# Cross-attention of a perceiver layer: the value product ahead of the scores on TensorE, low part and sums ahead of the scaled scores on VectorE

## The reference, cut to what matters

```
x = x + xattn(layernorm(x), ctx, lens, Wq, Wk, Wv, Wo, q_norm_w, k_norm_w)     # x [32, 64, 128], ctx [32, 1601, 128]

qh = rms_norm(heads(q @ Wq), q_norm_w);  kh = rms_norm(heads(kv @ Wk), k_norm_w);  vh = heads(kv @ Wv)   # 16 heads of 64
scores = where(mask, einsum('bhld,bhsd->bhls', qh, kh) / 8, NEG_INF)
o = einsum('bhls,bhsd->bhld', softmax(scores), vh)
return o.reshape(b, l, 1024) @ Wo
```

## Time and profile before

| what | value |
|---|---|
| median of 3 runs | 2734.34 us (2728.91 to 2734.52) |
| the profiled execution, its own time | 2733.9 us |
| its span, first to last instruction | 2732.0 us |
| PE busy | 2497.1 us, 91% |
| PEld / DVE / ACT / POOL busy | 78% / 76% / 51% / 45% |
| TensorE's granted clock, mean | 0.966 of full |

### The profile page before, as it was taken

How to read it: one execution, slowest core, us unless ns; L and a number is a source line. 1 busy time by engine, 2 the same in 40 slices (tenths; PEclk the granted TensorE clock), 3 DMA queues, 4 the chain that set the end, 5 groups by cost and what they waited for, 6 DMA issues and landing times. The chain is left out here.

```text
span 2732.0 us, 53851 instructions
## 1 busy us (share of the span) xinstructions
PE 2497.1 (91%) x16440; PEld 2131.2 (78%) x16440; DVE 2063.5 (76%) x3018; ACT 1395.2 (51%) x3048; POOL 1239.8 (45%) x638
## 2 busy tenths in 40 slices
PE   5979999999999999999999999999999868799842
PEld 3657888888888888888888888888888757677622
DVE  5679888888888888888888888888888501666567
ACT  4644555555555555555555555555555330465530
POOL 2313555555555555555555555555555630122245
PEclk7999999999999999999999999999999979899975
DMA  2331111111111111111111111111111035000000
GB/s 82 139 111 34 42 41 48 40 40 40 52 40 41 48 40 40 39 40 40 48 40 41 41 52 40 40 48 41 40 39 36 21 129 203 1 0 0 1 0 16
DMA packets 136733, 128.14 MB, mean 47 GB/s; under 512 B 9776, under 2 KB 119280, under 8 KB 136560
## 3 DMA queue, kind: packets, MB, share of 16 engines
q1 hardware_dynamic: 132080, 110.78, 12.9%
q10 hardware_dynamic: 4608, 16.78, 1.5%
HBM read 92.91 MB, written 34.60 MB: 47 GB/s over the span
## 5 line engine op out<-in xcount | busy, mean ns | idle before, releaser
L360 POOL TENSOR_TENSOR probs<-scores,best_all 128x1024 f32 (+2 forms) x416 | 985.4, 2373 | 950.2 <-DVE best L704 942.8
L886 PEld LDWEIGHTS u_ps<-rows,probs 128*128 128x128 f32 x6656 | 806.1, 192 | 53.4 <-issue 9.2
L689 DVE SCALAR_TENSOR_TENSOR scores<-s_ps,mask,rrms 128x512 f32 (+2 forms) x832 | 618.6, 745 | 272.8 <-PE s_ps L761 272.5
L886 PE MATMUL u_ps<-rows,probs 128*128 (+1 forms) x6656 | 811.0, 275 | 13.4 <-ACT probs L545 11.0
L545 ACT ACTIVATE probs<-probs 128x1024 f32<-128x1024 f32 (+1 forms) x416 | 439.6, 1057 | 421.4 <-POOL probs L360 417.5
L506 ACT ACTIVATE squares<-k_ps 128x512 f32<-128x512 f32 (+1 forms) x832 | 464.0, 597 | 201.0 <-PE k_ps L761 145.6
L665 DVE TENSOR_REDUCE ssq<-squares 128x16 f32<-128x1024 f32 (+1 forms) x416 | 502.1, 1207 | 0.0
L704 DVE TENSOR_TENSOR best<-best,scores 128x1024 f32<-128x1024 f32 (+1 forms) x352 | 467.7, 1329 | 0.3
L759 PE MATMUL k_ps<-w_hi,cT_hi 128*128 128x512 f32 (+1 forms) x832 | 362.5, 436 | 11.6 <-DVE cT_lo L659 11.6
L759 PE MATMUL s_ps<-q_hi,cT_hi 128*128 (+2 forms) x832 | 361.9, 435 | 3.5 <-ACT best_all L511 1.4
L761 PE MATMUL k_ps<-w_hi,cT_lo 128*128 128x512 f32 (+1 forms) x832 | 327.7, 394 | 0.0
(11 more groups left out here) (199 smaller groups left out, 2576.7 us busy)
## 6 DMA issues: line engine op xcount, KB each, us to landing
stage<-in_ctx SPq DMA_DIRECT2D x384, 64.0 KB, 1.7
rows<-in_ctx SPq DMA_DIRECT2D x32, 768.0 KB
queries<-probs SPq DMA_DIRECT2D x16, 1024.0 KB, 4.0
q_plain<-queries SPq DMA_DIRECT2D x32, 512.0 KB, 3.2
u_transposed<-uT_sb ACTq DMA_DIRECT2D x32, 512.0 KB, 2.7
a_uT<-u_transposed SPq DMA_DIRECT2D x16, 1024.0 KB, 4.7
a_wqkv<-in_L_attn_w_qkv SPq DMA_DIRECT2D x1, 1536.0 KB, 9.4
stage<-in_ctx SPq DMA_DIRECT2D x32, 32.5 KB
```

The lines of the kernel that those rows point to most:

```text
L360: pool.tensor_tensor(probs[0:r, slot_of(c, PRING), :], scores_at(b, c), best_all[0:r, bass.ds((b % 2) * HL, HL)], ALU.subtract).then_inc(s ...
L689: dve.scalar_tensor_tensor(out=scores_at(p, c, h * HALF, HALF).rearrange("p (h l) -> p h l", l=L), in0=s_ps[h][0:r, :].rearrange("p (h l) ...
L886: last = pe.matmul(u_ps[g // 3][:, at:at + UW], probs[0:r, s, g * P:(g + 1) * P], rows, start=(c == 0 and g % 3 == 0), stop=(c == NC - 1), ...
```

## The change

In PE's step `values` moves ahead of `score`. In DVE's step `split_lo` and then `sum_squares` move ahead of both `scale`, which now follow each other. The instructions and their waits are the same, and so are all buffers.

```diff
@@ DVE, step @@
                 if on.rows and c == 0:
                     keep_best(p - 1, n - 1, NC - 1)
+                if on.turn:
+                    split_lo(n + TURN_AHEAD, at_step(p, c, TURN_AHEAD)[1])
+                if on.keys:
+                    sum_squares(n + KEYS_AHEAD, at_step(p, c, KEYS_AHEAD)[1])
                 if on.scores:
                     scale(p, n, c, 0)
-                if on.turn:
-                    split_lo(n + TURN_AHEAD, at_step(p, c, TURN_AHEAD)[1])
-                if on.scores:
                     scale(p, n, c, 1)
-                if on.keys:
-                    sum_squares(n + KEYS_AHEAD, at_step(p, c, KEYS_AHEAD)[1])
@@ PE, step @@
                     turn(later, n + TURN_AHEAD, tile)
-                if on.scores:
-                    score(p, n, c)
                 if on.values:
                     vc = (c - LAG) % NC
                     values(p - 1 if c >= LAG else p - 2, n - NC - LAG, vc)
+                if on.scores:
+                    score(p, n, c)
```

## The result

| | before | after |
|---|---|---|
| median of 4 runs each | 2734.43 us (2728.91 to 2737.25) | 2916.56 us (2913.4 to 2920.85) |
| ratio | | 1.067, 95% interval 1.0648 to 1.0691 |
| the profiled execution / its span | 2733.9 / 2732.0 us | 2913.4 / 2911.5 us |
| granted clock, mean | 0.966 | 0.968 |

A forecast was written before the change was run, and what follows sets the result against it. PE, full in the dense loop, was taken as the bound. Stalls of 5.06 us in each of 29 batches (146.7), plus 0.6, 0.9 and 9.2, summed to 157.4 us, giving 2891 us; range 2838 to 2930 us.

The forecast's parts named there:

- The full PE with its gain of 0: Dense loop: PE is busy 500.00 of 500 us and the change removes no instruction, so nothing is gained.
- The third rival: Switch between product and value matmuls: not slower, some 0.09 us dead time saved a step, 37 us, 2697 us; 2%.
- the signs: PE in the loop: exponential row some 110 us, over 170 entries; busy about 92%; stalled `values` at K+2.0 to 2.3.
- E - 1.29: Value product in PE's step: stall in us from an exponential ending at E, with deadline 1.50 and restart 0.21.
- The four saves: ACT in c = 3, 4, 8, 9: saves delay the exponential; stalls 0.69 + 0.62 + 0.63 + 0.54 = 2.48 us a batch.
- the second rival: Plain steps stall too: hand-overs cost 0.05 us more each, 0.2 in six free steps, 35 us more, 2926 us; 15%.
- the first: Rival: only the saves and the division stall, 3.52 us a batch, 2842 us; 12%.
- The restart: PE's value product after a wait: 0.14 us to the first matmul plus 0.07 over 16; 0.21, bounds 0 to 0.21.
- VectorE's half at no cost: DVE's plain step: its moves cost nothing, covered by 0.87 us of slack before `scale` 0 can start.
- The reading as a wait for the port: DVE, c = 10: `keep_best` waits for POOL's `q_lo`, then runs whole; 2891 us, against 2907 with shared bandwidth.
- The stretch without `project`: Rest of p = 31: the chain, not PE, bounds; steps go from 3.81 to 4.65 us, 9.2 us over 11 steps.
- chain of 7.6: Rest of p = 31: us from `score` of c to `values` of c+2; with 1.7 added, two steps take 9.3.

## Why the prediction was right, and where it was too low

**What bounds and what gives way.** The full PE with its gain of 0 was right. Only c = 7 got shorter, by 0.11, and most of that is a boundary that moved. The two kernels with the later value product show it without stalls: c = 8, 9 and 10 take 5.04 + 5.11 + 4.76 = 14.91 us under PE's new order and 5.12 + 5.11 + 4.67 = 14.90 under the old one, so what the step with the first transposes gains the plain step behind them gives back. The third rival, a dead time that the switch between products would save, has nothing for it. Of the signs, the row behind the exponential had its 172 entries but 68.3 us, not 110, and PE's busy share fell to 95%, not 92: a modelled end of a matmul hides part of each stall. `values` came at K+2.0 to 2.1 in five of the seven steps, but at K+2.38 in c = 0 and 2.64 in c = 6.

**The deadline.** E - 1.29 held; E is the end of the exponential in its step, counted from K, the start of `project`. ACT's rows of c = 3 and c = 6:

```profile
1250.16 0.60 ACT L511 ACTIVATE best_all<-x_ps 128x512 f32 x1 [2.85 <-PE x_ps L863]
1250.66 1.05 ACT L545 ACTIVATE probs<-probs 128x1024 f32<-128x1024 f32 x1
...
1266.13 1.06 ACT L545 ACTIVATE probs<-probs 128x1024 f32<-128x1024 f32 x1 [2.96 <-POOL probs L360]
1267.09 2.15 ACT L519 ACTIVATE u_sb<-u_ps,inv_sum 128x128 f32<-128x128 f32 x8
```

In c = 3 the save pushes the exponential to 1251.71, K+1.98 as forecast, and the step grew 0.64 for 0.69. The four saves together cost 2.48 (0.64 + 0.67 + 0.60 + 0.57) for 2.48, c = 0 0.90 for 0.87. Each of the four is off by up to 0.05. The plain steps c = 5, 10 and 12, whose margin was put at 0.03, stayed at 4.68: the second rival is out, and so is the first, which gave 2842, as six exponentials a batch do wait.

**The restart.** It was the unknown price, put at 0.21 between 0 and 0.21. The first matmul follows the end of the exponential by 0.14 (1251.71 to 1251.85) and 16 take 2.05 for the 1.95 of c = 5: 0.24. From what the Trainium skill (TensorE: Matmul & The Clock Gate, "The mechanism") says on weight loads pulled ahead of matmuls in flight the forecast had drawn that it could be free, and the time 2848. The trace shows that it is not free here, where the weights themselves are what is awaited.

**VectorE's half at no cost: the step that failed.** The slack of 0.87 was right as a sum over the step, but the chain does not ask for a sum. DVE's rows of c = 10, 1 and 5, and POOL's of c = 10 and 5:

```profile
1219.44 1.70 DVE L704 TENSOR_TENSOR best<-best,scores 128x1024 f32<-128x1024 f32 x1
...
1239.67 0.68 DVE L708 TENSOR_REDUCE best_row<-x_ps 128x4 f32<-128x512 f32 x1
...
1260.45 1.43 DVE L689 SCALAR_TENSOR_TENSOR scores<-s_ps,mask,rrms 128x512 f32 x2 [0.47 <-PE s_ps L760]
1262.00 1.23 DVE L704 TENSOR_TENSOR best<-best,scores 128x1024 f32<-128x1024 f32 x1
```

```profile
1217.66 2.41 POOL L390 TENSOR_TENSOR q_lo<-q_plain,q_hi 128x1024 f32 x1
...
1263.71 2.39 POOL L360 TENSOR_TENSOR probs<-scores,best_all 128x1024 f32 x1 [3.63 <-DVE best L704]
```

- `keep_best` now stands directly behind the `scale` whose result it reads. It starts 1.55 behind the pair's start, not 2 x 0.66 = 1.32: at K+1.18, not K+1.00. `sum_squares` between the two had hidden the end of `scale`. In c = 5 that moves the shift and the exponential and with them the division of c = 6: 1.20 for 1.04. The running maximum in two halves gave this back (c = 6 in 5.77 us, 1.05 over before).
- `best_of_columns` in c = 1 starts at K+0.67, behind both scales. The transpose comes at K+1.60 for K+1.48, and the step pays 0.34 where 0 was forecast.
- c = 11: 0.69 for 0.55. The start of `keep_best` in c = 10, K+1.18 rather than 1.00, costs nothing by itself, as it meets `q_lo` on POOL and ends 1.07 behind it (1220.07 to 1221.14), as it did by 1.08 in the earlier trace rows. But the `keep_best` of c = 9 is late in the same way, the shift behind it too, and `q_lo` behind that ends at K+1.81 for the 1.70 of the forecast (whose own terms, 4.45 + 2.40 less a step of 5.21, give 1.64). The reading as a wait for the port, and not as shared bandwidth, was right, as the Trainium skill has it (SBUF — State Buffer, "SBUF: two separate sides").

The misses are 0.16 + 0.34 + 0.14 = 0.64 a batch, 29 x 0.64 = 18.6 us of the loop's 19.4; the other ten steps together are 0.02 below the forecast, c = 7 by 0.11 and the rest above or below by a few hundredths. VectorE's half alone, at 60 us, shows the same places larger, where no other wait has put PE back: c = 1 costs 0.82 there and 0.34 here, and the wait of c = 7 for `split_lo` is absent here. The parts do not add: 498 and 62 us alone against the runs of before beside them, 182 together. VectorE's half removes the wait for `split_lo` that TensorE's half makes in the plain steps (5.5 us for 4.68).

**The stretch without `project`.** 16.3 for 9.2, and the base of the 9.2 was misread. The forecast took the 3.81 us a step of the earlier trace rows for half of its chain of 7.6, though its own formula (less the score ahead of `values`) would have given 3.1. In the kernel before that stretch is a mean of two kinds of step: in four of the ten PE waits for a save and they take 4.55 to 4.80 us from `score` to `score`, in five nothing waits and they take 3.17 to 3.20:

```profile
2129.06 0.50 PE L759 MATMUL s_ps<-q_hi,cT_hi 128*128 128x512 f32 x1 [0.69 <-ACT best_all L511]
...
2132.26 0.48 PE L759 MATMUL s_ps<-q_hi,cT_hi 128*128 128x512 f32 x1
```

In the changed kernel the chain does decide: two neighbouring steps without another wait take 9.15 us (`score` at 2289.84 and 2298.99) and 9.12 (2316.25 and 2325.37), near the 9.3 of the forecast. So half of the formula held, and that its start agreed with the trace was luck. From c = 2 to c = 12 the step is 5.15 us in the mean, not 4.65. What the forecast had not are the division, at which one product waits 3.00 us, and value products that run slowly behind a wait. Two rows, and the windows of their 16 matmuls (columns as in the earlier trace rows):

```profile
2303.64 2.06 PE L885 MATMUL u_ps<-rows,probs 128*128 128x129 f32 x16 [3.00 <-ACT u_sb L519]
...
2312.89 3.61 PE L885 MATMUL u_ps<-rows,probs 128*128 128x129 f32 x16 [2.16 <-ACT probs L545]
```

```profile
2303.64:2305.70 2.06, 2.06 (x17) 2.06 (x18) 0.00 (x0) 1.56 (x6) 1.61 (x1) 1.00 0.03 6
2312.89:2316.50 3.61, 3.61 (x17) 3.61 (x18) 0.00 (x0) 0.00 (x0) 2.27 (x1) 0.54 0.02 5
```

The second ran at a granted clock of 0.54 and took 1.56 more than 2.05. Two more are like it: 3.22 us at 0.61 behind an idle 2.15, and 3.69 at 0.54 behind 2.51. The first, behind the longest wait of all, ran at the full clock.

**The sum.** The forecast was 25 us too low on the medians, and 27.6 on the two profiled executions without the stretch ahead (19.4 + 7.1 + 1.1 behind the last `values`). That 2916.56 lies in the range is in part luck: above 2907 the range was there for the plain steps that might stall, and they did not.

## What to carry to other kernels

When an order changes on a full engine, give each consumer its deadline and each producer its ready time, for every class of step apart, and then do the same for each buffer whose reader stands behind the moved work; a sum of busy times per step says nothing here, since the order was free in nine of 13 steps, and in four it cost 60 us. An instruction put directly behind the one that feeds it loses the overlap of neighbours (here 0.2 us of 1.3). Where a chain of hand-overs meets its deadline by hundredths, a step more of lag costs little and can gain: here it took back 123 of 182 us, and 0.3% in the kernel that had no visible wait.

## What the runs showed of the hardware that had not been expected

- Waits of PE of up to 1.0 us (the longest in its rows) in the loop of the changed kernel left the granted clock at 1.00 in the window from 500 to 1000 us. Idle times of 1.87 us (sums behind the scales) and of 2.16, 2.15 and 2.51 us (the stretch without `project`) were followed by 16 matmuls at a granted clock of 0.54 to 0.61, which took 3.22 to 3.69 us for 2.05. But behind an idle 3.00 us in the same stretch the clock was 1.00 and the 16 took 2.06. So the length of the one wait does not tell whether the clock falls, and these runs do not show what does.
- A small instruction of DVE with two SBUF inputs (128x144) took 1.49 us beside POOL's shift and 0.30 without: its size does not bound its cost. A large one (128x1024) that started while POOL's `q_lo` ran ended 1.07 to 1.08 us behind it, whether the two had overlapped by 1.30 us or by 0.63.
- A kernel's first stretch ends about 5.5 us earlier in some executions than in others; the traces taken do not say why.
